# Folding the read-out weights of a state-space scan into the scan's own tables, and building those tables inside the first expert layer

## The chip, the cores and the metric

One core of a Trainium2 chip. The time is device time of one execution in microseconds (us). The kernel before took 613.54 us, the median of 3 runs (612.56 to 614.28).

## The reference

4096 tokens of 256 numbers go through three layers, in fp32:

```
x = x + 0.5 * ffn(layernorm(x))        # 8 experts, one of them per token
x = x + ssm(layernorm(x))              # the recurrence
x = x + 0.5 * ffn(layernorm(x))        # the same experts again

ssm:  Bu_t = B_disc @ u_t              # 128 complex states
      h_t  = a_disc * h_{t-1} + Bu_t   # elementwise
      y_t  = Re(C @ h_t)
ffn:  e = argmax(softmax(x @ Wr)), p = its probability
      out = p * (gelu(x @ W1[e] + b1[e]) @ W2[e] + b2[e])    # 256 -> 1024 -> 256
```

## The kernel before

Everything stands in one program of five instruction streams that wait on one another's semaphores; the order on each engine is written out by hand. It has four stages.

**Entry** (to about 85 us): weights are loaded and split into two fp16 parts each, and the tokens are sorted by expert.

**First expert layer** (`ffn(1)`, about 85 to 303 us). 39 tiles, numbered q. 32 of them hold 128 tokens; seven narrow ones, of 112 down to 16 tokens, hold the rest of each expert. The narrow tiles of 80, 64, 48 and 32 tokens stand at q = 18, 23, 28 and 33, so between full ones, and those of 112, 96 and 16 tokens are the last three. For a tile TensorE turns the tokens (L1245), makes the first product (L1270, 48 matmuls) and the second (L1292 to L1294, 24 matmuls). In iteration q it issues: turn tile q+2, first product of q+1, second product of q. ScalarE does the gelu (L617). VectorE does in iteration q, in this order: `split_x(q+2)` (L950, what the first product of q+2 waits for), `split_h(q+1)` (L964 and L967 for each half, which wait for the gelu of q+1 and are waited for by the second product of q+1), and `result(q)` (L981 to L988: scale, add, statistics of the next layernorm). The result lies in one of two buffers `og`, and GpSimd scatters it to memory by an indirect DMA (L430); `result(q)` waits until the scatter of q-2 has landed. GpSimd also fetches the tokens of tile q+6 (L424).

**Recurrence** (about 303 to 375 us). The 4096 tokens are 8 chunks (`c`) of 512. The states are not complex numbers that turn but two real scans per chunk: the input is turned by a table `turn` (cosines and sines of the angle times the place in the chunk), scanned with the factor `rho` = |a_disc|, and turned back by a table `back`, which also holds B_disc's factor. VectorE does in chunk c: multiply `turn` by the input that TensorE made (L1121, 2 x 512), two scans (L1124), scores and `add_y` of chunk c-1 (L1096 to L1105), the product with `back` (L1133, 2 x 512), and the sum of the two halves into `hr` (L1136). GpSimd makes the start values of chunk c+1 from the ends of the scans (L468 to L474). TensorE does in chunk c: input of c+1 (`into_states`, L1372), turning of chunk c+2 (L1359), scores of chunk c from the normed tokens (L1387, which waits for `add_y(c-1)`), and the read-out of `hr` (L1404).

The tables are made on VectorE in `ffn(1)`: `double(n)` (L774 to L781) makes entries n to 2n of `turn` from the first n. Those for n = 1 to 32 run after `result(q)` for q = 4, 6, ..., 14; those for n = 64, 128 and 256 and the two `readout` calls, which make `back` (L783 to L788), run after the loop's last tile.

**Routing and second expert layer** (about 375 to 611 us): as the first, without tables and statistics.

## Time and profile before

| | |
|---|---|
| median of the timed runs | 613.54 us |
| the profiled execution | 613.17 us |
| its span, first to last instruction | 611.4 us |
| granted TensorE clock, mean | 0.926 of full |
| TensorE busy | 551.8 us, 90% |
| VectorE busy | 467.6 us, 76% |
| GpSimd busy | 288.1 us, 47% |
| stretch of the first expert layer | about 85 to 303 us |
| stretch of the recurrence, first multiply to last scores | 317.13 to 375.0 us |

PE is TensorE, PEld its weight loads, DVE VectorE, ACT ScalarE, POOL GpSimd, SP SyncE. "L1124" is line 1124 of the kernel before. `banks` is PSUM, and `weights_arena` the large buffer in which nearly all tiles lie. Durations of matmuls are modelled at their ends, so times between starts are the safer reading for TensorE.

### The profile page before, as it was taken

What the parts mean: (1) busy time and instruction counts of PE and PEld (TensorE: products, weight loads), DVE (VectorE), ACT (ScalarE), POOL (GpSimd) and SP (SyncE); (2) the same over time, 40 slices, a digit from 0 to 9 for tenths busy, and PEclk for the clock granted to TensorE, in tenths of its full rate; (3) what the DMA queues carried; (4) which work ended last, traced back from release to release, by engine and by line L of the source; (5) the groups of instructions that cost most, each with busy time, mean ns of one, the idle gap of its engine ahead of it and who ended that gap; (6) DMA issues with size and microseconds to landing.
All of it is one profiled execution on the core that took longest, in us unless ns stands there. A gap on an engine that the chain in (4) does not pass through costs nothing.

```text
span 611.4 us, 18700 instructions
## 1 busy us (share of the span) xinstructions
PE 551.8 (90%) x6548; PEld 508.6 (83%) x6548; DVE 467.6 (76%) x1007; ACT 409.8 (67%) x966; POOL 288.1 (47%) x326
## 2 busy tenths in 40 slices
PE   5992158999999999999989989699999999999996
PEld 5991047999999999999977767699999999999996
DVE  5789997888887788877749998666677666666674
ACT  3899977676667776676455662387766677766763
POOL 0025075655655555653245142655555555545532
PEclk9555569999999999999999996799999999999999
DMA  7999112211111121111081223111111112111210
GB/s 250 369 370 378 33 26 97 62 47 55 54 45 55 37 52 44 46 47 36 16 278 35 93 80 104 58 46 54 52 48 53 51 48 45 46 46 46 52 30 15
DMA packets 34873, 51.94 MB, mean 85 GB/s; under 512 B 6747, under 2 KB 27933, under 8 KB 34528
## 3 DMA queue, kind: packets, MB, share of 16 engines
q1 hardware_dynamic: 24800, 31.93, 15.3%
q0 software_dynamic: 9984, 18.83, 11.4%
q8 instruction: 56, 0.92, 0.6%
q14 instruction: 33, 0.27, 0.2%
HBM read 37.98 MB, written 14.59 MB: 86 GB/s over the span
## 4 chain that ended last, share of the span: by engine, by line
PE 67%; DVE 11%; issue 6%; DMA 6%; SPq 4%; POOL 4%; ACT 1%; POOLq 0%; DVEq 0%; ACTq 0%
PE banks L1270 30%; PE banks L1292 10%; PE banks L1293 10%; PE banks L1294 10%; DVE weights_arena L1124 3%; PE banks L1245 3%; DMA weights_arena<-L_attn_u 2%; PE banks L1200 2%; SPq L330 2%; DMA weights_arena<-x_after_ffn 2%; DVE weights_arena L1133 1%; POOL weights_arena L424 1%; DVE weights_arena L1121 1%; SPq L313 1%; DVE weights_arena L1105 1%
## 5 line engine op out<-in xcount | busy, mean ns | idle before, releaser
L617 ACT ACTIVATE weights_arena<-banks,b1t,inv 128x128 f32<-128x128 f32 (+7 forms) x624 | 220.1, 459 | 31.3 <-PE banks L1270 31.2
L1270 PE MATMUL banks<-weights_arena 128*128 128x128 f16 (+7 forms) x3744 | 207.0, 215 | 1.2 <-DVE weights_arena L950 1.1
L1270 PEld LDWEIGHTS banks<-weights_arena 128*128 x3744 | 199.9, 98 | 3.5 <-issue 2.5
L1292 PE MATMUL banks<-weights_arena 128*128 (+7 forms) x624 | 170.3, 273 | 0.2 <-issue 0.2
L1294 PE MATMUL banks<-weights_arena 128*128 (+7 forms) x624 | 170.2, 273 | 0.0
L1293 PE MATMUL banks<-weights_arena 128*128 (+7 forms) x624 | 170.2, 273 | 0.0
L964 DVE TENSOR_SCALAR weights_arena<-weights_arena,hscale 128x512 f16<-128x512 f32 (+5 forms) x156 | 74.7, 479 | 76.0 <-ACT weights_arena L617 75.2
L967 DVE SCALAR_TENSOR_TENSOR weights_arena<-weights_arena,hscale 128x512 f16<-128x512 f32 (+5 forms) x156 | 109.9, 704 | 5.6
L591 ACT ACTIVATE weights_arena<-banks,xscale 128x256 f16<-128x256 f32 (+7 forms) x78 | 35.5, 455 | 90.7 <-PE banks L1245 90.7
L424 POOL DMA_INDIRECT recf<-records,sorti x78 | 76.9, 986 | 23.8 <-issue 23.8
L430 POOL DMA_INDIRECT out<-weights_arena,sorti x39 | 39.5, 1014 | 78.4 <-DVE weights_arena L984 70.6
L430 POOL DMA_INDIRECT x_after_ffn<-weights_arena,sorti x39 | 39.9, 1024 | 77.0 <-DVE weights_arena L988 68.6
L1292 PEld LDWEIGHTS banks<-weights_arena 128*128 128x128 f16 (+7 forms) x624 | 62.3, 100 | 7.0 <-issue 0.7
L1294 PEld LDWEIGHTS banks<-weights_arena 128*128 128x128 f16 (+7 forms) x624 | 62.3, 100 | 6.5
L1293 PEld LDWEIGHTS banks<-weights_arena 128*128 128x128 f16 (+7 forms) x624 | 62.3, 100 | 5.7
L424 POOL DMA_INDIRECT weights_arena<-L_attn_u,sorti x39 | 46.2, 1184 | 29.0 <-DVE sorti L928 17.4
L575 ACT ACTIVATE weights_arena<-weights_arena,recf 128x256 f32<-128x256 f32 (+7 forms) x78 | 46.0, 590 | 8.8 <-DMA recf<-records,sorti 8.8
L981 DVE SCALAR_TENSOR_TENSOR weights_arena<-banks,inv,weights_arena 128x256 f32<-128x256 f32 (+7 forms) x78 | 37.6, 483 | 16.1 <-issue 5.9
L424 POOL DMA_INDIRECT weights_arena<-x_after_ssm,sorti x39 | 40.0, 1026 | 15.1 <-issue 11.6
L950 DVE SCALAR_TENSOR_TENSOR weights_arena<-banks,xscale,weights_arena 128x256 f16<-128x256 f32 (+7 forms) x78 | 35.6, 457 | 7.8 <-ACT weights_arena L591 7.0
L984 DVE SCALAR_TENSOR_TENSOR weights_arena<-weights_arena,recf 128x256 f32<-128x256 f32 (+7 forms) x78 | 37.8, 484 | 2.8
L729 DVE SCALAR_TENSOR_TENSOR weights_arena<-weights_arena,wscale 128x2048 f16<-128x2048 f32 x16 | 37.1, 2341 | 2.3 <-ACT weights_arena L516 2.3
(216 smaller groups left out, 639.1 us busy)
## 6 DMA issues: line engine op xcount, KB each, us to landing
weights_arena<-L_ffn_W SPq DMA_DIRECT2D x16, 1024.0 KB, 12.6
weights_arena<-x_after_ffn SPq DMA_DIRECT2D x8, 516.0 KB, 8.4
weights_arena<-L_attn_u SPq DMA_DIRECT2D x8, 512.0 KB, 10.8
x_after_ssm<-weights_arena SPq DMA_DIRECT2D x8, 512.0 KB, 2.9
weights_arena<-L_ffn_b SPq DMA_DIRECT2D x2, 1024.0 KB, 5.2
recf<-records,sorti POOLq DMA_INDIRECT x78, 2.5
weights_arena<-L_attn_u,sorti POOLq DMA_INDIRECT x39, 3.3
x_after_ffn<-weights_arena,sorti POOLq DMA_INDIRECT x39, 2.5
```

Source lines behind the costliest of these rows:

```text
L424: pool.indirect_dma_start(to, None, source, bass.IndirectOffsetOnAxis(ap=sorti[:, slot(q), index:index + 1].bitcast(U32), axis=0)).then_in ...
L430: pool.indirect_dma_start(dst, bass.IndirectOffsetOnAxis(ap=sorti[:, slot(q), 2:3].bitcast(U32), axis=0), og[q % 2] if ph == 1 else og[q % ...
L575: act.activation(xng[q % 2][0:w], xg[q % RING][0:w], ACT.Identity, bias=recf[0:w, q % RING, 0:1], scale=recf[0:w, q % RING, 1:2]).then_inc ...
L617: last = act.activation(hb[q % 2][:, f, 0:width(q)], src, ACT.Gelu, bias=b1t[:, bass.ds(e * FC + f, 1)], scale=inv1[:, bass.ds(e, 1)])
L964: dve.tensor_scalar(hs[q % 2][:, 0, f, of], hb[q % 2][:, f, of], sc, None, ALU.mult) \
L967: dve.scalar_tensor_tensor(hs[q % 2][:, 1, f, of], hb[q % 2][:, f, of], sc, hs[q % 2][:, 0, f, of], ALU.mult, ALU.subtract).then_inc(s["hs ...
L981: dve.scalar_tensor_tensor(o, acc, i2, b2b[0:w, bass.ds(e * D, D)], ALU.mult, ALU.add) \
L984: last = dve.scalar_tensor_tensor(o, o, recf[0:w, q % RING, 2:3], xg[q % RING][0:w], ALU.mult, ALU.add)
L1270: last = pe.matmul(acc[:, f * P:f * P + n_cols], weights[wpart * DC + d], xts[q % 2][:, xpart, d, 0:n_cols], start=(n == 0), stop=(n == 5))
L1292: pe.matmul(acc, hs[q % 2][:, 0, f, of], high, start=(f == 0), stop=False)
L1293: pe.matmul(acc, hs[q % 2][:, 0, f, of], low, start=False, stop=False)
L1294: last = pe.matmul(acc, hs[q % 2][:, 1, f, of], high, start=False, stop=(f == FC - 1))
```

## The change

1. The factors of `back` are applied inside the scans. The table `turn` is multiplied by the read-out weight w_t of its place, and the constant factor `rho` of the scan becomes a table of `rho * w_t / w_(t-1)` (in `back`). What the scan gives is then already weighted, and the product with `back` (L1133) is gone. `hr` is their sum.
2. `hr` of chunk c is made right after the scans of c, ahead of the scores and `add_y` of c-1. As `hr` now reads `zz` itself, the next multiply into `zz` also waits for it (`s_hr`).
3. The start values of the next chunk divide the weights out again: GpSimd's four products use four numbers of a small table `carry`.
4. For this the tables need the inverses of the weights. Weights nearer to zero than 1e-15 get 1e-12 added. All of it, with the doublings of 64, 128 and 256 and both `readout` calls, is done by `tables_after(q)` after `result(q)` for q = 16 to 34 of the first expert layer; after its last tile only a memset of `state` is left.
5. `og` has six buffers (RING) where it had two, in both expert layers; `result(q)` waits for the scatter of q-6.

```diff
-                                            og[q % 2] if ph == 1 else og[q % 2][:, 0:D], None, ...
+                                            og[q % RING] if ph == 1 else og[q % RING][:, 0:D], None, ...
...
-                pool.tensor_tensor(ev[:, 18:19], zr, cl, ALU.mult)
+                pool.tensor_tensor(ev[:, 18:19], zr, carry[:, 0:1], ALU.mult)
...
+            def away_from_zero(part):
+                tmp, weight = aa[:, part, :], back[:, part, :]
+                link(dve.tensor_tensor(tmp, weight, weight, ALU.mult))
+                link(dve.tensor_scalar(tmp, tmp, NEAR_ZERO ** 2, None, ALU.is_lt))
+                link(dve.scalar_tensor_tensor(weight, tmp, STAND_IN, weight, ALU.mult, ALU.add))
+            def inverse_of_both(quarter):
+                of = slice(quarter * CH // 4, (quarter + 1) * CH // 4)
+                link(dve.tensor_tensor(aa[:, 0, of], back[:, 0, of], back[:, 1, of], ALU.mult))
+                link(dve.reciprocal(aa[:, 0, of], aa[:, 0, of]))
+            def inverses(part):
+                link(dve.tensor_tensor(inverse[:, part, :], back[:, 1 - part, :], aa[:, 0, :], ALU.mult))
+            def carries():
+                last = CH - 1
+                ends = inverse[:, :, last]
+                dve.tensor_scalar(carry[:, 0:2], ends, turn[:, 0, last:CH], None, ALU.mult)
+                link(dve.tensor_scalar(carry[:, 2:4], ends, turn[:, 1, last:CH], None, ALU.mult))
+            def weighted_turn(part):
+                link(dve.tensor_tensor(turn[:, part, :], turn[:, part, :], back[:, part, :], ALU.mult))
+            def steps(part):
+                tmp = aa[:, part, :]
+                link(dve.scalar_tensor_tensor(tmp[:, 1:CH], back[:, part, 1:CH], rho[:], inverse[:, part, 0:CH - 1],
+                                              ALU.mult, ALU.mult))
+                link(dve.tensor_scalar(tmp[:, 0:1], back[:, part, 0:1], rho[:], None, ALU.mult))
+                link(dve.tensor_copy(back[:, part, :], tmp))
+            def tables_after(q):
+                if 4 <= q < 16 and q % 2 == 0:
+                    double(1 << (q // 2 - 2))
+                elif q == 16:
+                    double(CH // 8)
+                elif q == 18:
+                    double(CH // 4)
+                elif q in (19, 20):
+                    double(CH // 2, CH // 4 * (q - 19), CH // 4 * (q - 18))
+                elif q in (21, 22):
+                    readout(q - 21)
+                elif q in (23, 24):
+                    away_from_zero(q - 23)
+                elif 25 <= q < 29:
+                    inverse_of_both(q - 25)
+                elif q in (29, 30):
+                    inverses(q - 29)
+                elif q in (31, 32):
+                    if q == 31:
+                        carries()
+                    weighted_turn(q - 31)
+                elif q in (33, 34):
+                    steps(q - 33)
...
-                    if q >= 2:
-                        dve.wait_ge(s["scat"][(q - 2) % RING], (q - 2) // RING * 16 + 16)
+                    if q >= RING:
+                        dve.wait_ge(s["scat"][q % RING], q // RING * 16)
...
-                        if 4 <= q < 16 and q % 2 == 0:
-                            double(1 << (q // 2 - 2))
+                        tables_after(q)
                 if ph == 1:
-                    for n in (CH // 8, CH // 4, CH // 2):
-                        double(n)
-                    dve.memset(state[:], 0.0)
-                    readout(0)
-                    readout(1)
+                    link(dve.memset(state[:], 0.0))
...
                 if c >= 1:
+                    dve.wait_ge(s_hr, c)
                     dve.wait_ge(s_state, c)
                 dve.tensor_tensor(zz, turn[:], both(bank[2]), ALU.mult).then_inc(s_mod, 1)
                 dve.wait_ge(s_mod, c + 1)
                 for part_of in range(2):
-                    scan = dve.tensor_tensor_scan(zz[:, part_of, :], rho[:].to_broadcast([P, CH]), zz[:, part_of, :],
+                    scan = dve.tensor_tensor_scan(zz[:, part_of, :], back[:, part_of, :], zz[:, part_of, :],
                                                   state[:, part_of:part_of + 1], ALU.mult, ALU.add)
                 scan.then_inc(s_scan, 1)
+                if c >= 2:
+                    dve.wait_ge(s_y, c - 1)
+                dve.wait_ge(s_scan, c + 1)
+                dve.tensor_tensor(hr[c % 2], zz[:, 0, :], zz[:, 1, :], ALU.add).then_inc(s_hr, 1)
                 if c >= 1:
                     logits_of(c - 1)
                     add_y(c - 1)
                 else:
                     negative_means(len(BATCHES) - 1)
-                dve.wait_ge(s_scan, c + 1)
-                link(dve.tensor_tensor(zb, zz, back[:], ALU.mult))
-                if c >= 2:
-                    dve.wait_ge(s_y, c - 1)
-                dve.tensor_tensor(hr[c % 2], zb[:, 0, :], zb[:, 1, :], ALU.add).then_inc(s_hr, 1)
```

`link` makes the next VectorE instruction wait for the end of the one it wraps. `double` takes a range now, so that the doubling of 256 runs in two halves of 128 entries.

## Rows read from the trace of the kernel before

**Rows 1.** The page, part 1: busy us (share), instructions.
```profile
PE 551.8 (90%) x6548; PEld 508.6 (83%) x6548; DVE 467.6 (76%) x1007; ACT 409.8 (67%) x966; POOL 288.1 (47%) x326
```

**Rows 2.** Timeline of TensorE, first expert layer: start us, duration us, engine, line, operation.
```profile
210.02 2.85 PE L1270 MATMUL banks<-weights_arena 128*128 128x128 f16 x48
...
215.55 1.56 PE L1270 MATMUL banks<-weights_arena 128*128 128x64 f16 x48
...
219.79 2.84 PE L1270 MATMUL banks<-weights_arena 128*128 128x128 f16 x48
```

**Rows 3.** Timeline of VectorE, same stretch; in brackets idle us before, and the releaser.
```profile
207.72 0.49 DVE L964 TENSOR_SCALAR weights_arena<-weights_arena,hscale 128x512 f16<-128x512 f32 x1 [0.81 <-ACT weights_arena L617]
...
211.94 0.35 DVE L950 SCALAR_TENSOR_TENSOR weights_arena<-banks,xscale,weights_arena 128x128 f16<-128x128 f32 x1
...
217.86 0.48 DVE L950 SCALAR_TENSOR_TENSOR weights_arena<-banks,xscale,weights_arena 128x256 f16<-128x256 f32 x1
```

**Rows 4.** Timeline of VectorE, recurrence: one chunk, and the last chunk's multiply.
```profile
337.36 1.21 DVE L1121 TENSOR_TENSOR weights_arena<-turn,banks 128x1024 f32<-128x1024 f32 x1
338.61 2.46 DVE L1124 TENSOR_TENSOR_SCAN weights_arena<-rho,state,weights_arena 128x512 f32<-128x512 f32 x2
...
341.36 1.21 DVE L1105 TENSOR_TENSOR weights_arena<-weights_arena,banks 128x1024 f32<-128x1024 f32 x1
342.49 1.22 DVE L1133 TENSOR_TENSOR weights_arena<-weights_arena,back 128x1024 f32<-128x1024 f32 x1
343.74 0.69 DVE L1136 TENSOR_TENSOR weights_arena<-weights_arena 128x512 f32<-128x512 f32 x1
...
365.32 1.22 DVE L1121 TENSOR_TENSOR weights_arena<-turn,banks 128x1024 f32<-128x1024 f32 x1
```

**Rows 5.** Timeline of TensorE, recurrence: chunk 0, then a later chunk.
```profile
320.91 1.04 PE L1359 MATMUL banks<-ident,weights_arena 128*128 128x128 f32 x8
321.78 1.85 PE L1387 MATMUL banks<-wrc,weights_arena 128*128 128x8 f32 x16
323.52 2.06 PE L1404 MATMUL banks<-ct,weights_arena 128*128 128x265 f32 x8
...
344.50 2.05 PE L1404 MATMUL banks<-ct,weights_arena 128*128 128x265 f32 x8
346.38 1.88 PE L1372 MATMUL banks<-weights_arena,bt 128*128 128x512 f32 x4
348.10 1.04 PE L1359 MATMUL banks<-ident,weights_arena 128*128 128x128 f32 x8
```

**Rows 6.** Timeline of GpSimd, start value of chunk 1.
```profile
321.62 1.16 POOL L473 TENSOR_TENSOR state<-ev 128x1 f32<-128x1 f32 x1
```

**Rows 7.** Timeline of VectorE after the first expert layer: `double` and `readout`.
```profile
303.71 0.29 DVE L778 TENSOR_SCALAR back<-turn 128x128 f32<-128x128 f32 x1
...
304.88 0.35 DVE L778 TENSOR_SCALAR back<-turn 128x256 f32<-128x256 f32 x1
...
306.46 0.48 DVE L787 TENSOR_SCALAR weights_arena<-turn,ev 128x512 f32<-128x512 f32 x1
...
307.76 0.49 DVE L787 TENSOR_SCALAR weights_arena<-turn,ev 128x512 f32<-128x512 f32 x1
```

**Rows 8.** Groups of VectorE by line and form: count, busy us, mean ns, idle before.
```profile
L722 DVE RECIPROCAL wscale<-bound 128x2 f32<-128x2 f32 x8 | 1.3, 166 | 0.3
L916 DVE RECIPROCAL records<-records 128x32 f32<-128x32 f32 x2 | 0.7, 356 | 0.1
```

**Rows 9.** VectorE waiting ahead of L964, 188.9 to 290 us: total us, times.
```profile
  ACT weights_arena L617: 12.5, 17
```

**Rows 10.** Timelines, end of the first expert layer: VectorE's result of the 96-token tile, TensorE.
```profile
299.52 0.48 DVE L981 SCALAR_TENSOR_TENSOR weights_arena<-banks,inv,weights_arena 96x256 f32<-96x256 f32 x1 [1.86 <-DMA x_after_ffn<-weights_arena,sorti]
...
300.66 10.98 PE L1178 MATMUL banks<-iota_r,ident 128*128 128x128 f32 x96
```

**Rows 11.** Busy time of TensorE by stretch: us, busy, granted clock, DMA share, GB/s.
```profile
368.00:370.00 2.00, 2.00 (x12) 0.50 0.00 0
```

More of the change, by code:

```diff
@@ L55 @@
 TINY = 1e-30
+NEAR_ZERO = 1e-15
+STAND_IN = 1e-12
 WE = DC * F
@@ L119, in macaron @@
         state = sb("state", [P, 2])
+        carry = sb("carry", [P, 4])
         wsum = sb("wsum", [P, NW])
@@ L177, in macaron @@
         hs = [view(4096 + k * 1024, 2, FC, P, dt=F16) for k in range(2)]
-        og = [view(6144 + k * RW, RW) for k in range(2)]
+        og = [view(6144 + k * RW, RW) for k in range(RING)]
         xg = [view(8192 + k * D, D) for k in range(RING)]
@@ L181, in macaron @@
         xts = [view(10240 + k * 256, 2, DC, P, dt=F16) for k in range(2)]
-        outcols = [view(6912 + k * D, DC, P) for k in range(2)]
+        outcols = [view(12288 + k * D, DC, P) for k in range(2)]
         xs = view(0, NJ, RW)
@@ L188, in macaron @@
         zz = view(NJ * RW + 2 * CT * D + 2 * DC * CH, 2, CH)
-        zb = view(NJ * RW + 2 * CT * D + 2 * DC * CH + 2 * CH, 2, CH)
+        inverse = view(NJ * RW + 2 * CT * D + 2 * DC * CH + 2 * CH, 2, CH)
         hr = [view(NJ * RW + 2 * CT * D + 2 * DC * CH + 4 * CH + k * CH, CH) for k in range(2)]
@@ L430, in scatter @@
                     pool.indirect_dma_start(dst, bass.IndirectOffsetOnAxis(ap=sorti[:, slot(q), 2:3].bitcast(U32), axis=0),
-                                            og[q % 2] if ph == 1 else og[q % 2][:, 0:D], None, bounds_check=T - 1, oob_is_err=False) \
+                                            og[q % RING] if ph == 1 else og[q % RING][:, 0:D], None, bounds_check=T - 1, oob_is_err=False) \
                         .then_inc(s["scat"][q % RING], 16)
@@ L467, in _ @@
                 pool.wait_ge(s_scan, c + 1)
-                pool.tensor_tensor(ev[:, 18:19], zr, cl, ALU.mult)
-                pool.tensor_tensor(ev[:, 19:20], zi, cl, ALU.mult)
-                pool.tensor_tensor(ev[:, 20:21], zi, sl, ALU.mult)
-                pool.tensor_tensor(ev[:, 21:22], zr, sl, ALU.mult).then_inc(s_prod, 1)
+                pool.tensor_tensor(ev[:, 18:19], zr, carry[:, 0:1], ALU.mult)
+                pool.tensor_tensor(ev[:, 19:20], zi, carry[:, 1:2], ALU.mult)
+                pool.tensor_tensor(ev[:, 20:21], zi, carry[:, 3:4], ALU.mult)
+                pool.tensor_tensor(ev[:, 21:22], zr, carry[:, 2:3], ALU.mult).then_inc(s_prod, 1)
                 pool.wait_ge(s_prod, c + 1)
@@ L772, in rotation, with double @@
                 link(dve.tensor_scalar(turn[:, 1, 0:1], col(11), col(13), None, ALU.mult))
-            def double(n):
-                c0, s0 = turn[:, 0, 0:n], turn[:, 1, 0:n]
+            def double(n, begin=0, end=None):
+                end = n if end is None else end
+                c0, s0 = turn[:, 0, begin:end], turn[:, 1, begin:end]
                 cn, sn = turn[:, 0, n - 1:n], turn[:, 1, n - 1:n]
-                dve.tensor_scalar(back[:, 0, 0:n], s0, sn, None, ALU.mult)
-                link(dve.tensor_scalar(back[:, 1, 0:n], c0, sn, None, ALU.mult))
-                dve.scalar_tensor_tensor(turn[:, 0, n:2 * n], c0, cn, back[:, 0, 0:n], ALU.mult, ALU.subtract)
-                link(dve.scalar_tensor_tensor(turn[:, 1, n:2 * n], s0, cn, back[:, 1, 0:n], ALU.mult, ALU.add))
+                dve.tensor_scalar(back[:, 0, begin:end], s0, sn, None, ALU.mult)
+                link(dve.tensor_scalar(back[:, 1, begin:end], c0, sn, None, ALU.mult))
+                dve.scalar_tensor_tensor(turn[:, 0, n + begin:n + end], c0, cn, back[:, 0, begin:end], ALU.mult, ALU.subtract)
+                link(dve.scalar_tensor_tensor(turn[:, 1, n + begin:n + end], s0, cn, back[:, 1, begin:end], ALU.mult, ALU.add))
             def readout(part):
@@ L975, in result @@
                     dve.wait_ge(s["m2"], q + 1)
[L976 to L977 removed]
+                    if q >= RING:
+                        dve.wait_ge(s["scat"][q % RING], q // RING * 16)
                     w = width(q)
[L979 removed]
+                    o, acc = og[q % RING][0:w, 0:D], bank[4 + q % 2][0:w, 0:D]
                     i2 = inv2[0:w, bass.ds(e, 1)]
@@ L987, in result @@
                         link(dve.bn_stats(stats[0:w, q % 2, :], o))
-                        last = dve.bn_aggr(og[q % 2][0:w, D:D + 2], stats[0:w, q % 2, :])
+                        last = dve.bn_aggr(og[q % RING][0:w, D:D + 2], stats[0:w, q % 2, :])
                     last.then_inc(s["o"], 1)
```

2 lines of the change are left out of this document (removed).

## The prediction, made before the changed kernel was run

> **What bounds the kernel now.** I read the busy times first [rows 1]: TensorE is busy for 90% of the span, VectorE for 76%. That is a mean over stages, so I went on to the timelines of the two stages that the change touches.
>
> In the first expert layer TensorE sets the pace. The first products start at 210.02 and 215.55 (5.53 us for a full tile), and 4.24 us later at 219.79 behind the 64-token tile [rows 2]. VectorE needs less: of a full tile's 5.5 us it waits 0.81 for the gelu [rows 3]. `split_x` runs ahead of its product. The one at 211.94 ends at 212.29, 3.26 us before the product at 215.55 that needs it; behind a narrow tile the lead is short, 218.34 against 219.79, so 1.45 us [rows 2, 3]. These leads are the cover for anything that makes VectorE late.
>
> In the recurrence VectorE sets the pace, with no idle time that a row names: multiply 1.25 us (start to start), two scans 2.46, scores and `add_y` to 342.49, the product with `back` 1.25, `hr` 0.69. From the multiply at 337.36 (chunk 3) to the one at 365.32 (chunk 7) four periods pass, 6.99 us each [rows 4]. TensorE has slack, but not much. Its four groups take, start to start, 1.88 (read-out), 1.72 (input), 0.87 (turning, from chunk 0, where the next group doesn't wait) and 1.74 (scores): 6.21 us [rows 5].
>
> **The recurrence after the change.** The product with `back` goes: 1.25 us per chunk, so VectorE's own period becomes 5.74. TensorE's is 6.21 and is late next, so it gives the new pace. I walked both through the chunks. The read-out of chunk 0 stays at 323.52, as the scores ahead of it already fill TensorE [rows 5]. `hr` is ready earlier, but the first `add_y` comes after it and holds the next scores: multiply of chunk 1 at about 322.5 (its start value, ready at 322.9 behind an operation of 1.22, now comes behind `hr`'s 0.69 [rows 4, 6]), its `hr` done 4.35 later, scores and `add_y` 1.6 more, 328.4; the read-out of chunk 1 then starts near 330.3, where it now would be 323.52 + 6.99 = 330.5. From there the period is 6.21: read-outs at 336.5, 342.7, 348.9, 355.1. The multiply of chunk 7 needs the input product, which starts 1.88 after the read-out of chunk 5 and, with its end and the semaphore, is there some 2.1 later: 359.1. Before it was 365.32, gain 6.2. Behind it lie only VectorE's scans, `hr`, `add_y` and routing, shorter by one more 1.25: **gain 7.4 us**. Were VectorE the bound throughout, it would be 8 x 1.25 = 10.0. If TensorE's period were 6.4 it would be 6.4.
>
> The moved `hr` and the new wait for it cost nothing: `add_y` stands between `hr` and the next multiply. The start value must be there too. GpSimd's six small products usually take 1.1 us behind the scans, but while VectorE ran a product of two SBUF operands one of them took 1.16 instead of some 0.2 [rows 6]. `hr` is such an operation and now starts together with them: 0.69 + 1.1 = 1.8 us, against 0.61 + 0.37 + 1.13 = 2.1 until the next multiply. It is hidden, by 0.3; past the first chunk TensorE gives another 0.4.
>
> The scans get a table where they had one broadcast number. No row shows a scan so fed. A product of two fp32 operands takes 0.69 for 512 against 0.48 with one [rows 4, 7], so up to 0.21 per scan, 0.42 per chunk; a gain has no reason. I take 0: a scan runs at 1.23 per 512 [rows 4], slower than either. The other end gives a VectorE period of 6.16, still under TensorE's 6.21, and only the last chunk's 0.4 and the first's are paid, about 1 us.
>
> The Trainium skill ("DVE: opcode table, instruction layouts, handler registers and perf-mode slots", section 6) says that the built-in scan runs at half throughput because its result is fed back. The two scans' 2.46 us for 1024 elements, against 1.21 for the multiply of as many [rows 4], agree; by that rule the second table is hidden, by the other end it costs the 1 us above.
>
> **The tables in the first expert layer.** Each call is priced to the next start in its chain, with 0.1 for restarting `split_x` behind a chained end:
> - q = 16: doubling of 64, between 0.9 and 1.17: 1.0. q = 18, 19, 20: doublings over 128 entries, 304.88 - 303.71 = 1.17, so 1.27 each [rows 7].
> - q = 21, 22: `readout`, 307.76 - 306.46 = 1.30, so 1.4 each [rows 7].
> - q = 23, 24: product 0.69, comparison 0.48, and the multiply-add 0.75 that is in `readout`'s 1.30; with gaps 2.1 each.
> - q = 25 to 28: product of 128 (0.28) and a reciprocal of 128. The trace has reciprocals of 2 columns at 0.166 and of 32 at 0.356 [rows 8]: 6.3 ns a column, 0.96 us for 128. 1.4 each. Below, a plain operation's 0.29 for 128 [rows 7] would make 0.7; above, 1.6.
> - q = 29, 30 0.8 each; q = 31 1.15; q = 32 0.8; q = 33, 34 (multiply 0.75, a small one, copy 0.48) 1.6 each.
>
> The sum is 24.2 us in 19 tiles. Before, the part of it that already existed (three doublings and two `readout`s) ran after the layer while TensorE waited for the reload of the tokens, and was hidden. Room in the layer: VectorE waits for the gelu 12.5 us in this stretch [rows 9], and I add an estimate of 0.1 for each of these 17 waits, where it could start at once: 14 to 15 us. The difference is some 9.5 us.
>
> The leads don't store that. I carried the lateness from tile to tile, adding each call, subtracting each wait, and letting TensorE wait where lateness exceeds the lead less an estimated 0.4 for restarting it. It passes until q = 20 (2.5 late against 2.8); then TensorE waits behind the narrow tile at 23 (1.5), for tiles 26, 27, 28 (1.0, 1.0, 0.7), behind 28 (2.0), for 31 (0.3), behind 33 (1.2) and for 37 (0.3): **8.0 us**, and 0.9 of lateness goes into the tail. Work 10% less or more makes it 5.8 or 10.4; 20% less, 3.9.
>
> **The six buffers.** Only one wait for a scatter shows, at the 96-token tile: 1.86 us [rows 10]. Behind it the last result follows, and everything waits for its scatter. Two results of 1.7 us from 299.52 end at 302.9. TensorE's last product ends at 300.66 [rows 10], so the last result can end at 302.4: gain 0.5, of which the lateness may eat some. I take 0.3. In the second layer the last results wait for TensorE: 0. What ran after the layer (6.3 us) frees VectorE at a time when nothing needs it: 0.
>
> **The sum.** +8.0 - 0.3 - 7.4 = +0.3 us. The profiled execution took 613.17, its span 611.4 with 1.8 around it, 0.4 under the median; on the median 613.5 the sum gives 613.8.
>
> **The rivals.**
> - *The tables fit.* If VectorE does the calls in 80% of my price (a quicker reciprocal, short chained gaps), TensorE waits 3.9 us, not 8.0. Time 609.7. For it: q = 14's doubling today costs nothing at all. Against it: the account of VectorE's time doesn't close unless much of the 24.2 us is overpriced. A clock that holds to the end of the recurrence (now 0.50 at 368 [rows 11]) could add up to 1 us. Chance, for all that ends under 611.7: 0.32.
> - *TensorE's clock falls in the expert layer* (the slower side). Now it is at the full level through the layer, without idle time. With eight waits of 0.3 to 2 us it may fall as it does near 368, after a stretch with gaps and small products. At 0.50 each 8 us of products take 8 more, of which VectorE's lateness pays back its wait, some 4: 613.8 + 4 = 617.8. It decides from the first wait over 1 us, at tile 24. Against it: in the recurrence the clock stays at the full level with two gaps in each 7 us. Chance 0.12.
> - *The calls cost 10% to 15% more* (two-operand products held up, reciprocals at 1.2): TensorE waits 10.4 or more: 616.2. Chance, with the scans' 1 us, 0.17.
> - *The change doesn't do what it says:* scans fed by a table run at 1.44 each. As worked out, 614.8, because TensorE hides most. This lies inside the likeliest case's own range.
>
> On the second of these the Trainium skill ("TensorE: Matmul & The Clock Gate", section on HAM oscillation) warns that idle gaps between bursts of matmuls throttle the engine again; by that rule the time is the 617.8 of that case. No row here shows a fall inside an expert layer.
>
> **How the numbers follow.** About 0.3% (1.8 us) is what a measurement of this kernel can tell from no change. The likeliest case, the two sides cancel, has 0.39 and the range 611.7 to 615.4. Faster is the first rival, 0.32 (its bound with both ends: 3.9 waits and 8.5 gain, 608.6). Slower is 0.12 + 0.17 = 0.29, to 618. The range 609.5 to 618 leaves out the ends of both.
>
> **What would show it.** No group of products with `back` in the recurrence, periods of 6.2 there with TensorE waiting nowhere; the last scores about 7.4 us closer to the first multiply. In the first expert layer VectorE without waits for the gelu from q = 18 on, and TensorE's first products waiting for `split_x`, most of all behind the narrow tiles; the layer's last product some 8 us later. The prediction is wrong if TensorE's products keep their 5.5 us through q = 34, or if the recurrence runs at 5.8.

## The result, and the profile after

The kernel after takes 615.45 us (median of 15 runs, 613.48 to 617.39), the one before, measured beside it, 613.24 (15 runs). The ratio is 1.0032 with a 95% interval of 1.0020 to 1.0044: slower, by 2.2 us, just beyond the 0.3% that I had called the limit of what can be told. I had forecast +0.3 us, and 615.45 lies 0.05 above the range 611.7 to 615.4 that I had given to the likeliest case. Single executions of one kernel differ by 1 to 2 us with how TensorE's clock behaved in the first 20 us, which the last section shows.

The profiled execution took 616.36 us. Its page, the span and part 1 (busy us, share, instructions), to be held against [rows 1]:

```profile
span 614.6 us, 18732 instructions
PE 551.8 (90%) x6548; PEld 508.2 (83%) x6548; DVE 471.9 (77%) x1029; ACT 410.8 (67%) x966; POOL 289.9 (47%) x326
```

Nothing there says what happened: the busy times are the same within 1%, though eight products of 1.22 us are gone and a table is built. The stages say it. I cut both spans at the same instructions, from the timelines (us; the differences are my subtraction):

| stretch | before | after | difference | forecast |
|---|---|---|---|---|
| start to the first product of tile 2 (q = 2) | 99.88 | 101.46 | +1.58 | 0 |
| first expert layer, from there to TensorE's last product | 200.78 | 208.47 | +7.69 | +8.0 |
| from there to the first multiply of the recurrence | 16.47 | 16.37 | -0.10 | -0.3 |
| first multiply to the last (chunk 0 to 7) | 48.19 | 43.70 | -4.49 | -6.2 |
| last multiply to the last scores | 9.41 | 8.37 | -1.04 | -1.25 |
| routing, to the first product of the second expert layer | 22.38 | 21.84 | -0.54 | 0 |
| to the end | 214.29 | 214.39 | +0.10 | 0 |
| span | 611.4 | 614.6 | +3.2 | +0.3 |

The first row is not the change: nothing ahead of that product was edited, and the same stretch takes 99.81 or 101.27 us in two kernels below whose code there is identical (experiments 2 and 3; the last section gives the cause). What is left, 1.6 us, is the change by the traces; the medians say 2.2.

**The layer.** TensorE's first products of tiles 22, 23 (the narrow one), 24 and 26 (the first of them answers to the one at 210.02 in [rows 2]); the bracket is idle time and releaser:

```profile
211.61 2.85 PE L1329 MATMUL banks<-weights_arena 128*128 128x128 f16 x48
217.13 1.61 PE L1329 MATMUL banks<-weights_arena 128*128 128x64 f16 x48
223.21 2.85 PE L1329 MATMUL banks<-weights_arena 128*128 128x128 f16 x48 [1.62 <-DVE weights_arena L1014]
...
235.44 2.85 PE L1329 MATMUL banks<-weights_arena 128*128 128x128 f16 x48 [0.75 <-DVE weights_arena L1014]
```

Behind the narrow tile the next product comes 6.08 us later, where it was 4.24 [rows 2]: 1.84 more. The bracket names `split_x` (L1014) as what it waited for. The waits of the whole layer, after (us in all, times, longest):

```profile
PE banks L1329 <- DVE weights_arena L1014: 6.9, 6, 1.9
DVE weights_arena L1028 <- ACT weights_arena L619: 8.4, 8, 3.6
```

Of the first line 0.5 us, one wait near the layer's start, stood in before too. The second line is VectorE's spare time in 100 to 312 us; by the same view of 190 to 305 alone it has none left, where before had the 12.5 us of [rows 9]. The groups of VectorE in 190 to 305 us say it too (idle before it, at the end of the line):

```profile
L1028 DVE TENSOR_SCALAR weights_arena<-weights_arena,hscale 128x512 f16<-128x512 f32 (+6 forms) x40 | 19.4, 484 | 0.4 <-issue 0.3
```

**The recurrence.** VectorE, the last periods before and after the wait (start, duration, idle and releaser):

```profile
349.81 1.22 DVE L1181 TENSOR_TENSOR weights_arena<-turn,banks 128x1024 f32<-128x1024 f32 x1
351.06 2.46 DVE L1184 TENSOR_TENSOR_SCAN weights_arena<-back,state,weights_arena 128x512 f32<-128x512 f32 x2
...
355.97 1.22 DVE L1181 TENSOR_TENSOR weights_arena<-turn,banks 128x1024 f32<-128x1024 f32 x1
...
362.14 1.22 DVE L1181 TENSOR_TENSOR weights_arena<-turn,banks 128x1024 f32<-128x1024 f32 x1
363.39 2.46 DVE L1184 TENSOR_TENSOR_SCAN weights_arena<-back,state,weights_arena 128x512 f32<-128x512 f32 x2
...
370.00 1.22 DVE L1181 TENSOR_TENSOR weights_arena<-turn,banks 128x1024 f32<-128x1024 f32 x1 [1.80 <-POOL state L476]
```

The period is 6.16 to 6.17 us, where it was 6.99 [rows 4]. The scan that reads a table takes 2.46 for two, as before. But the last multiply comes 7.86 after the one before it, and waits 1.80 us for the start value. TensorE's groups run back to back (the transposes and scores of the chunk, left out here, fill 361.94 to 364.52):

```profile
358.35 2.03 PE L1463 MATMUL banks<-ct,weights_arena 128*128 128x265 f32 x8
360.22 1.88 PE L1431 MATMUL banks<-weights_arena,bt 128*128 128x512 f32 x4
...
364.52 2.03 PE L1463 MATMUL banks<-ct,weights_arena 128*128 128x265 f32 x8
```

364.52 - 358.35 = 6.17: TensorE sets the pace of the recurrence now. VectorE is close behind it: from its multiply at 355.97 to the end of `add_y` at 362.04 it takes 6.07, and the next multiply starts at 362.14, when the input product (360.22 + 1.88 = 362.10) is there. What held the start value is on GpSimd:

```profile
363.68 1.00 POOL L460 TENSOR_SCALAR m<-m 128x16 f32<-128x16 f32 x1 [2.44 <-ACT banks L661]
364.77 3.80 POOL L461 TENSOR_TENSOR records<-m,mhalf 128x16 f32<-128x16 f32 x1
368.64 0.23 POOL L462 TENSOR_TENSOR records<-nmean,records 128x16 f32<-128x16 f32 x1
368.82 0.19 POOL L470 TENSOR_TENSOR ev<-weights_arena,carry 128x1 f32<-128x1 f32 x1
...
369.68 0.19 POOL L476 TENSOR_TENSOR state<-ev 128x1 f32<-128x1 f32 x1
```

These first three are `second_norm`, the norm factors of the first half of the tokens, put on GpSimd's queue ahead of the start value of chunk 7. The scans it needs had ended at 365.85; it could begin only at 368.82. Before, the same three instructions (L457 to L459 there) stood in the same place of the queue:

```profile
356.82 0.94 POOL L457 TENSOR_SCALAR m<-m 128x16 f32<-128x16 f32 x1 [0.67 <-ACT banks L659]
357.84 3.35 POOL L458 TENSOR_TENSOR records<-m,mhalf 128x16 f32<-128x16 f32 x1
361.27 0.80 POOL L459 TENSOR_TENSOR records<-nmean,records 128x16 f32<-128x16 f32 x1
...
362.97 0.19 POOL L474 TENSOR_TENSOR state<-ev 128x1 f32<-128x1 f32 x1
```

They ended at 362.07, and the scans of that chunk at 362.04, so they held up nothing. The start value was ready at 363.16 and its multiply ran at 365.32 [rows 4], 2.2 us later, and no list of waits of the multiply named GpSimd.

Why are they 3 us later against the scans in after? They start when ScalarE has the squares that they need. TensorE's input product of chunk 6 and the last of these squares, in before, and then the last of the squares in after:

```profile
353.37 1.88 PE L1372 MATMUL banks<-weights_arena,bt 128*128 128x512 f32 x4
356.54 0.19 ACT L659 ACTIVATION_READ_ACCUMULATOR banks<-weights_arena,nmean 128x1 f32 x1
```

```profile
363.40 0.20 ACT L661 ACTIVATION_READ_ACCUMULATOR banks<-weights_arena,nmean 128x1 f32 x1
```

In before the squares were ready 1.6 us ahead of the multiply of chunk 6 (356.73 against 358.33), in after 1.5 behind it (363.60 against 362.14). ScalarE does them behind its copies of TensorE's results, so it keeps step with TensorE; and TensorE lost its lead over VectorE: its input product ended 3.1 us ahead of that multiply in before (355.25), and 0.04 ahead of it in after (362.10).

### The profile page after: what moved, and what is told of

Read it like the earlier page. It is cut to its first block, busy times and chain, and to the rows that moved or that the text cites. A ratio compares the mean times of both kernels' runs of the same rounds, so it can differ in the third digit from the quotient of the medians.

```text
span 614.6 us, 18732 instructions
## 1 busy us (share of the span) xinstructions
PE 551.8 (90%) x6548; PEld 508.2 (83%) x6548; DVE 471.9 (77%) x1029; ACT 410.8 (67%) x966; POOL 289.9 (47%) x326
## 4 chain that ended last, share of the span: by engine, by line
PE 70%; DVE 11%; issue 6%; POOL 5%; DMA 3%; ACT 2%; DVEq 1%; SPq 1%; ACTq 0%; POOLq 0%
PE banks L1329 27%; PE banks L1351 10%; PE banks L1353 9%; PE banks L1352 9%; PE banks L1259 4%; PE banks L1304 2%; PE banks L1231 2%; PE banks L1431 1%; POOL weights_arena L427 1%; DVE weights_arena L1031 1%; PE banks L1446 1%; DVE weights_arena L1028 1%; DMA recf<-records,sorti 1%; PE banks L1463 1%; DMA weights_arena<-x_after_ffn 1%
## 5 line engine op out<-in xcount | busy, mean ns | idle before, releaser
L1014 DVE SCALAR_TENSOR_TENSOR weights_arena<-banks,xscale,weights_arena 128x256 f16<-128x256 f32 (+7 forms) x78 | 35.6, 456 | 10.3 <-ACT weights_arena L593 6.9
```

## The experiments

All were measured beside the kernel before, whose median was 614.20 in the set of experiments 1 to 4 (28 runs), 613.21 in that of 5 to 8 (23) and 614.58 in that of 9 and 10 (17). The experiments have 4 to 12 runs each. Every ratio is to it. My account has two claims: the tables cost 7 to 8 us because VectorE is late behind narrow tiles, and the missing gain of the recurrence is `second_norm`. The rivals: each call costs TensorE its time wherever it stands; and the recurrence lost its time to `hr` and the new order.

**1. `second_norm` one chunk later.**

```diff
-                if c == NC - 3:
+                if c == NC - 2:
                     pool.wait_ge(s_sq, NC // 2)
                     second_norm(slice(0, NJ // 2))
```

> The changed kernel, but GpSimd makes the first half of the second norm's factors behind the start value of chunk 7, not ahead of it. Theory A (that work of some 5 us, which fitted into a period of 7 us, now holds up the start value by the 1.80 us that VectorE waited ahead of the last multiply): the last multiply comes 43.70 - 1.8 = 41.9 us after the first, the wait is gone, and the time is 1.5 to 1.8 us under the changed kernel's 615.45: 613.8. Rival B (VectorE would wait for TensorE's input product there anyway): the wait changes its releaser, under 0.3 us gained.

613.57 us, ratio 0.9984 (0.9969 to 0.9998). From the first multiply to the last it is now 41.80 us, where after has 43.70 and my walk had 41.97. GpSimd in this kernel, last chunks: the start value first, the norm factors behind it.

```profile
364.85 0.19 POOL L470 TENSOR_TENSOR ev<-weights_arena,carry 128x1 f32<-128x1 f32 x1 [4.69 <-DVE weights_arena L1184]
364.99 0.64 POOL L471 TENSOR_TENSOR ev<-weights_arena,carry 128x1 f32<-128x1 f32 x1
...
366.13 0.19 POOL L476 TENSOR_TENSOR state<-ev 128x1 f32<-128x1 f32 x1
366.41 0.21 POOL L460 TENSOR_SCALAR m<-m 128x16 f32<-128x16 f32 x1
366.71 2.91 POOL L461 TENSOR_TENSOR records<-m,mhalf 128x16 f32<-128x16 f32 x1
369.70 1.27 POOL L462 TENSOR_TENSOR records<-nmean,records 128x16 f32<-128x16 f32 x1
```

So 1.9 us of the recurrence were this wait. Nothing else was edited. The start value is ready at 366.32, 0.9 us ahead of its multiply at 367.22: of the 2.2 us of room in before, 0.9 are left.

**2. The table calls spread over the layer from q = 1.**

```diff
-                if 4 <= q < 16 and q % 2 == 0:
-                    double(1 << (q // 2 - 2))
-                ...
+                if 1 <= q < 9:
+                    double(1 << (q - 1))
+                elif q in (9, 10):
+                    double(CH // 2, CH // 4 * (q - 9), CH // 4 * (q - 8))
+                elif q in (12, 13):
+                    readout(q - 12)
+                elif q in (15, 17):
+                    away_from_zero((q - 15) // 2)
+                elif q in (19, 20, 22, 24):
+                    inverse_of_both((19, 20, 22, 24).index(q))
+                elif q in (25, 27):
+                    inverses((q - 25) // 2)
+                elif q == 29:
+                    carries()
+                    weighted_turn(0)
+                elif q == 30:
+                    weighted_turn(1)
+                elif q == NT - 1:
+                    steps(0)
+                    steps(1)
```

> The changed kernel with the same tables, but the calls begin at q = 1 instead of 4, the wide doublings at 7 to 10 instead of 16 to 20, and the last step (two calls) comes after the layer's last tile. Theory A (the loss in the first expert layer is an account of VectorE's time: 24 us of calls in tiles that have 15 us of room; the tiles from 1 to 15 have some 0.9 us each that stood empty): TensorE waits 1 to 2 us in place of 7.7, the stretch from its second first-product to its last product is 190.5 against 196.6, and the time is some 6 us under 615.45: 609.5. Rival B (each call costs TensorE time by itself, by its chained gaps or by memory contention, wherever it stands): the stretch stays at 196 or more and the time at 615.

612.42 us, ratio 0.9961 (0.9945 to 0.9978). The layer takes 204.20 us, 4.3 less than after and 3.4 more than before. The calls are the same, only their places differ, so "each costs TensorE its time wherever it stands" falls. But I had expected 6. Waits were left at eight tiles (11 to 24), by the starts of the first products 0.83 us at the largest and 3.4 in all. The prices are hardly to blame, as in after the calls came out as forecast (next section); so the account had too much room or too long leads in these tiles, and which of the two is not shown.

**3. Both.** The edits of 1 and 2 together.

> Both edits together: GpSimd's norm factors behind the last start value, and the table calls spread from q = 1. Theory A: the two add up, 615.45 - 6 - 1.7 = 607.8, so 5.5 under the kernel before. Rival B (a saving in the recurrence is given back by the routing behind it): 609.5, as the spreading alone.

611.01 us, ratio 0.9942 (0.9921 to 0.9964), where the sum of the two had promised 607.8. The layer is 204.11, as in 2. The recurrence shows something new: 45.16 us from the first multiply to the last, not 41.8. TensorE there (start, duration), and then by stretch (length, busy, granted clock, share and GB/s of DMA):

```profile
327.86 2.03 PE L1461 MATMUL banks<-ct,weights_arena 128*128 128x265 f32 x8
...
335.27 3.88 PE L1461 MATMUL banks<-ct,weights_arena 128*128 128x265 f32 x8
338.94 3.11 PE L1429 MATMUL banks<-weights_arena,bt 128*128 128x512 f32 x4
```

```profile
332.00:336.00 4.00, 3.33 (x23) 0.82 0.38 131
336.00:340.00 4.00, 4.00 (x10) 0.50 0.00 0
340.00:344.00 4.00, 4.00 (x24) 0.82 0.39 131
```

The granted clock fell from 2.4 to 1.2 GHz for some 7 us, and the read-out took 3.88 us for 2.03. As TensorE sets the pace now, that is 3.4 us of this execution. Most runs can't have had it: of the twelve, four (the profiled one, 613.17, among them) took 613.2 to 613.5 and the other eight 607.7 to 611.7, and the median lies 1.4 under experiment 2, near the 1.9 of `second_norm`.

**4. The tables alone:** the layer of after, the recurrence of before. The last four calls (`weighted_turn` and `steps`, two each) write to a place that nothing reads.

```diff
-                link(dve.tensor_tensor(turn[:, part, :], turn[:, part, :], back[:, part, :], ALU.mult))
+                link(dve.tensor_tensor(unused[:, part, :], turn[:, part, :], back[:, part, :], ALU.mult))
...
-                link(dve.tensor_copy(back[:, part, :], tmp))
+                link(dve.tensor_copy(unused[:, part, :], tmp))
...
+                link(dve.tensor_tensor(zb, zz, back[:], ALU.mult))
```

> The kernel before in its recurrence (product with back, old carries, old order), with the changed kernel's table calls at the same tiles and the six buffers; the last table writes go to an unused buffer. Theory A (the tables cost 7.7 us in the first expert layer, and the recurrence gave back 5.5): stretch of the first expert layer 196.6, recurrence with periods of 6.99, time 613.24 + 7.7 - 0.3 = 620.6. Rival B (part of the loss is from elsewhere in the change, such as six buffers or code layout): the layer shows less than 196, the time is under 619.

621.18 us (4 runs), ratio 1.0105 (1.0075 to 1.0135): 7.0 us slower by the medians. The layer takes 208.38, the recurrence 48.20, each as in the kernel that it comes from.

**5. The change without its tables.** The calls from q = 16 on are memsets of the three tables, so the recurrence computes with other numbers.

```diff
                 elif q == 16:
-                    double(CH // 8)
+                    link(dve.memset(turn[:, :, CH // 8:CH], 0.5))
                 elif q == 18:
-                    double(CH // 4)
+                    link(dve.memset(back[:], 0.5))
...
```

> The changed kernel without the table calls from q = 16 on: three memsets stand in for them, and the tables hold a constant, so the output of the recurrence is another; what is measured is the time of everything else. Theory A (the layer's 7.7 us are these calls alone): the first expert layer is as long as in the kernel before, the recurrence keeps the changed kernel's 43.7 us from the first to the last multiply, time 615.45 - 7.7 = 607.8. Rival (part of the layer's loss is due to the six buffers or another change): over 609.

608.50 us, ratio 0.9914 (0.9891 to 0.9938). The layer is 200.78, as before to the last digit, and the recurrence 43.49. All four runs are of the slower of the two kinds in the last section; against the ten runs of before of that kind in this set (614.40) they are 5.9 us faster, which is what the stages give, 4.7 in the recurrence and 1.0 behind it. (The trace is of the slowest of the four, and has 1.5 us more in the first tile of the second expert layer, as that of experiment 2 has and no other.) 4 and 5 together: the tables cost what the layer grew by, 7.6 to 7.7 us, and the rest of the change gives back 5.9.

**6. Six result buffers alone**, on the kernel before.

```diff
-        og = [view(6144 + k * RW, RW) for k in range(2)]
+        og = [view(6144 + k * RW, RW) for k in range(RING)]
...
-                    if q >= 2:
-                        dve.wait_ge(s["scat"][(q - 2) % RING], (q - 2) // RING * 16 + 16)
+                    if q >= RING:
+                        dve.wait_ge(s["scat"][q % RING], q // RING * 16)
```

> The kernel before with six result buffers and nothing else. Theory A: only the wait of 1.86 us at the 96-token tile goes, and TensorE's last product then bounds the last result, so the reload begins 0.3 to 0.4 us earlier: 613.24 - 0.3 = 612.9, same within the measurement. Rival (the whole wait of 1.86 us is gained): 611.4.

613.36 us, ratio 1.0000 (0.9986 to 1.0015). From the last product to the first multiply its trace has 16.19 us, 0.28 less than before, which is the size of my term; the comparison can't show so little. (Its trace has 10.71 us from the last multiply to the last scores, where before has 9.41: its granted clock was 0.51 in 364 to 380 us.)

**7. `hr` in its old place**, behind `add_y`, all else as in after.

```diff
-                ...
-                dve.tensor_tensor(hr[c % 2], zz[:, 0, :], zz[:, 1, :], ALU.add).then_inc(s_hr, 1)
                 if c >= 1:
                     logits_of(c - 1)
                     add_y(c - 1)
                 ...
+                dve.tensor_tensor(hr[c % 2], zz[:, 0, :], zz[:, 1, :], ALU.add).then_inc(s_hr, 1)
```

> The changed kernel with hr made behind the scores and add_y of the chunk before, its old place. Theory A (TensorE sets the period of 6.17 us and needs hr only some 4 us after the scans, while the early hr mainly holds up add_y): the periods stay at 6.2 and the time within 0.5 us of 615.45. Rival (the early hr is what lets TensorE run without gaps): periods of 6.5 and more, over 617.

613.17 us, ratio 0.9993 (0.9979 to 1.0006), so some 2 us under after. I had not expected that. The stages give 1.2 of it: 42.71 to the last multiply, 8.20 behind it. The periods end at 6.17 as in after (the early ones are 0.9 longer in all than in experiment 1); what differs is `second_norm`:

```profile
362.85 0.21 POOL L460 TENSOR_SCALAR m<-m 128x16 f32<-128x16 f32 x1 [2.29 <-ACT banks L661]
363.14 2.92 POOL L461 TENSOR_TENSOR records<-m,mhalf 128x16 f32<-128x16 f32 x1
366.14 0.24 POOL L462 TENSOR_TENSOR records<-nmean,records 128x16 f32<-128x16 f32 x1
```

3.5 us instead of 5.2, and the last multiply waits for nothing: `hr` ends at 367.97, the start value is ready before it, the multiply runs at 368.06. `second_norm` starts during VectorE's multiply of 361.89 and not inside a scan; the last section says why that matters. The other 1 us of the medians' difference is in none of these stages and stays open; in the two traces 0.75 of it lies ahead of tile 2, where the code is the same.

**8. The calls fitted to the spare time**, and `second_norm` later. Twenty calls go to places with room by the account, and the last five run behind the last tile, while the reload of the tokens is under way.

```diff
-                ...
+                calls = [lambda k=k: double(1 << k) for k in range(8)]
+                ...
+                places = (1, 2, 3, 4, 5, 6, 8, 9, 11, 13, 14, 17, 19, 22, 25, 28, 29, 32, 33, 34)
+                if q in places:
+                    calls[places.index(q)]()
+                elif q == NT - 1:
+                    carries()
+                    for part in range(2):
+                        weighted_turn(part)
+                    for part in range(2):
+                        steps(part)
```

> GpSimd's norm factors behind the last start value, and the table calls placed by the account of lateness: 20 calls at q = 1 to 34 so that none pushes VectorE past its leads, with 0.15 us more per call than priced, and the five last (5 us) behind the layer's last tile, where VectorE waits 6.9 us for the reload. Theory A: TensorE waits nowhere in the first expert layer (length as before the change, 7.7 us under the changed kernel's), the recurrence runs as in the first of these experiments (41.8 us to the last multiply): 615.45 - 7.7 - 1.9 = 605.9. Rival (the account is too coarse, as the spread version's 3.4 us of waits against 1.8 show): 2 us of waits are left, 608. A half-rate stretch of TensorE inside the recurrence, as one traced run of the second kind had, would add up to 3.4 us to single runs of either.

605.15 us (5 runs), ratio 0.9870 (0.9847 to 0.9893): faster than before and than every kernel so far. The medians differ by 8.1 us; four of the five runs are of the faster kind of the last section, and against the twelve runs of before of that kind (612.64) their median, 605.11, is 7.5 lower. The layer is 200.75 us, the recurrence 42.17. TensorE's products around the narrow tile keep the distances of [rows 2], 5.53 and 4.24:

```profile
211.06 2.85 PE L1322 MATMUL banks<-weights_arena 128*128 128x128 f16 x48
216.59 1.56 PE L1322 MATMUL banks<-weights_arena 128*128 128x64 f16 x48
220.83 2.84 PE L1322 MATMUL banks<-weights_arena 128*128 128x128 f16 x48
```

And behind the layer VectorE ends the last table and then still waits for the reload:

```profile
307.83 0.43 DVE L827 COPY back<-weights_arena 128x512 f32<-128x512 f32 x1
...
310.36 0.20 DVE L1165 TENSOR_SCALAR nb<-weights_arena 128x4 f32<-128x4 f32 x1 [1.98 <-DMA weights_arena<-x_after_ffn]
```

**9. Experiment 8 with `hr` in its old place**, by the edit of 7.

> The fitted version (20 calls where the account has room, five behind the layer, GpSimd's norm factors behind the last start value), with hr made behind add_y, in its old place. Theory C (the changed kernel with hr in its old place gained 1.2 us in its trace because the norm factors on GpSimd ran 3.2 us there and 5.0 with the early hr, and so held up the last start value less; with the factors moved away nothing is left to gain): within 0.5 us of the fitted version's 605.15. Rival (the late hr gains by itself, through the start values' products that it no longer stretches): 603.5 to 604.

605.65 us (6 runs), ratio 0.9854 (0.9827 to 0.9880). The same as 8 within the intervals. So no gain from the place of `hr` can be told once `second_norm` is out of the way; what it gave in 7 came, as far as the stages show it, by way of that queue. (Its profiled execution had a granted clock of 0.60 in 320 to 324 us, and 44.31 us to the last multiply.)

**10. `second_norm` later in the kernel before**, by the edit of 1.

> The kernel before with GpSimd's first norm factors behind the start value of chunk 7 and nothing else. Theory A (in a period of 6.99 us that work was hidden: the start value was ready 2.2 us before the multiply): no change, 613.2. Rival (the work cost something there too): 612 or less.

614.79 us, ratio 1.0005 (0.9987 to 1.0024), and 48.17 us to the last multiply, where before has 48.19. In the kernel before the place of these three instructions costs nothing. The change made it cost 1.9 us.

## Why the prediction was right or wrong

**The tables: right, for the reason given.** +7.69 us against +8.0. The calls from q = 16 to 34, each taken from the last instruction of `result` to the next `split_x` and less the same distance in before, add up to 23.5 us, where I had 24.2; none is more than 0.13 off. The starts of the first products show where (my subtraction against before): tile 24, behind the narrow one, 1.84 (forecast 1.5), 26 0.92 (1.0), 27 1.05 (1.0), 28 0.25 (0.7), 29 2.04 (2.0), 31 none (0.3), 34 1.32 (1.2), 37 0.25 (0.3). The account of lateness against lead holds here, though in experiment 2 it was 1.6 us too hopeful, and experiment 8, placed by it with 0.15 us more per call, took all of the waits away. Of the prices the one from furthest off held: the reciprocal of 128, worked out at 0.96 from [rows 8]. VectorE in after:

```profile
246.09 0.95 DVE L804 RECIPROCAL weights_arena<-weights_arena 128x128 f32<-128x128 f32 x1
```

**The pace of the recurrence: right.** TensorE is late next, at 6.17 (forecast 6.21). VectorE's own 5.74 was too low: its chain fills 6.07 of the 6.17, because `hr`, now right behind the scans, starts 0.1 us after their end, where scores started ahead of it. TensorE hid that. The scans cost nothing more; the first two multiplies lie 5.46 apart (5.37), the second with 0.9 us of waiting for its start value, which `hr` holds up. Without the wait of the last chunk the stretch is 41.80 (41.97).

**What failed is one step:** "Behind it lie only VectorE's scans, `hr`, `add_y` and routing", with the start value that "is hidden, by 0.3; past the first chunk TensorE gives another 0.4". I had priced GpSimd's six small products and not read what else stood on its queue. `second_norm` took 5.2 us there (356.82 to 362.07) and held up nothing, since it ended with the scans. In after it ends 3.0 us behind them, because the squares it needs come later against VectorE, and the start value's room is down from 2.2 us to 0.9; 1.80 us came out. The forecast of -6.2 became -4.49. Put into my sum, the 1.9 us make +2.2. That this is also the difference of the medians is partly luck: the stages of the two traces, without the first, add up to 1.6, as routing gave 0.54 that I had not forecast and the layer, the buffers and the tail were each off by 0.2 to 0.3. Experiment 1 shows the step alone, 8 and 9 without the other loss, and 10 that in the kernel before it costs nothing.

**The tail: 0.2 short.** 8.37 for 9.41 is 1.04, where I had 1.25.

**The buffers: of no effect that can be told.** -0.10 in after, -0.28 alone in experiment 6, where I said 0.3. In after the lateness of VectorE may take back part: it ends the last result 1.87 us after TensorE's last product.

**Routing: not forecast.** -0.54 us. The granted clock is 0.50 in its first 2.3 us in before and in its first 0.7 in after; how much of the 0.54 that makes is not shown. I had put up to 1 us of this into the rival "the tables fit".

**The rivals.** *The tables fit* did not happen in the kernel as changed, as the calls cost 3% less than priced and not 20% less; but it is possible, as experiment 8 shows. *TensorE's clock falls in the expert layer* did not happen. Its granted clock from 209 to 262 us, with 5.3 us of waits in it:

```profile
209.00:262.00 53.00, 47.69 (x657) 1.00 0.16 43
```

The section of the Trainium skill that I had set beside it ("TensorE: Matmul & The Clock Gate", on HAM oscillation) warns of idle gaps between bursts of matmuls, and I had read 617.8 out of it. Its own case has waits for DMA, longer than any wait of this layer; gaps of up to 2.0 us did not lower the clock in any layer profiled here, so that use of it was too wide, and longer gaps no run here tests. The fall that did come (experiment 3) was in the recurrence, in small products. *The calls cost 10% to 15% more* was near the truth in time (616.2) and not in cause: they cost 3% less. *Scans at 1.44* did not happen.

## What to carry to other kernels

When a stage gets a shorter period, list everything that stands on every engine's queue inside it, once-only work too, with what it waits for and its slack against the consumer: what was hidden by 2.2 us of slack names itself in no list of waits. When the bound moves from one engine to another, the old lead of the new one is gone (3.1 us here), and all that keeps step with it comes later against the rest. Work given to an engine that runs ahead of a bottleneck costs nothing up to its lead and its full time beyond, so it belongs in many small places ahead of the wide tiles, and what is left over behind the last one, where a reload covers it. And when a saving moves the bound to TensorE, its clock becomes part of the price.

## What the runs showed of the hardware that I had not expected

**GpSimd is held where it starts inside a VectorE operation with two SBUF operands.** In after, L460 starts at 363.68, inside the first scan (363.39 to about 364.62), and takes 1.00, up to 364.68; the same instruction takes 0.21 in experiment 1. L461, started at 364.77 inside the second scan (to 365.85), takes 3.80 for 2.91. In experiment 1 L462 starts at 369.70 and ends at 370.97, with this scan:

```profile
368.48 2.46 DVE L1184 TENSOR_TENSOR_SCAN weights_arena<-back,state,weights_arena 128x512 f32<-128x512 f32 x2
```

which ends at 370.94. And L471 takes 0.64 for 0.19 when `hr` runs. In experiment 7 L461 started 0.01 us ahead of the scans and took 2.92 right through them, and L460 took 0.21 beside a multiply whose second operand is in PSUM. The Trainium skill ("SBUF — State Buffer", section "SBUF: two separate sides") says that the two engines share a pair of ports as an exclusive lock, which a VectorE operation with two SBUF inputs takes against a GpSimd operation that reads SBUF. The trace agrees for GpSimd, in the kernel before as well: L459 starts at 361.27 inside a scan, takes 0.80, and ends at 362.07, where the scans end at 362.04. The page's other half, that VectorE is blocked when GpSimd starts first, is not what the trace shows: in experiment 1 L461 ran from 366.71 to 369.62, and the scans that start inside it, at 368.48, kept their 2.46. The measurement decides.

**One stretch of full clock at the start makes two kinds of execution.** The stretch up to tile 2 takes 99.81 to 100.16 us in the six profiled executions whose mean granted clock is 0.92 to 0.93, and 100.71 to 101.46 in the six with 0.99. So those with the higher mean are the slower, by 1.2 us from median to median. The timed runs say the same of one kernel: before's with the higher mean are 1.0, 1.8 and 2.2 us slower than its others in the three sets. TensorE's scores of 16 products in before, at 12 us, at 25 us and at the end of the recurrence, where the granted clock is 0.50 [rows 11]:

```profile
12.16 1.93 PE L1200 MATMUL banks<-wrc,weights_arena 128*128 128x8 f32 x16
...
24.74 3.42 PE L1200 MATMUL banks<-wrc,weights_arena 128*128 128x8 f32 x16
...
367.88 3.42 PE L1387 MATMUL banks<-wrc,weights_arena 128*128 128x8 f32 x16
```

And the same scores in after:

```profile
13.23 3.56 PE L1259 MATMUL banks<-wrc,weights_arena 128*128 128x8 f32 x16
...
28.41 3.42 PE L1259 MATMUL banks<-wrc,weights_arena 128*128 128x8 f32 x16
```

By stretch (length, then busy us and instructions of PE, PEld, DVE, ACT and POOL, then the granted clock), before and after:

```profile
20.00:40.00 20.00, 18.61 (x88) 18.12 (x88) 15.12 (x43) 18.25 (x20) 0.00 (x0) 0.50 1.08 366
```

```profile
20.00:40.00 20.00, 20.00 (x97) 20.00 (x98) 14.81 (x43) 18.95 (x20) 0.00 (x0) 1.00 1.08 365
```

3.42 us is the duration at 0.50, and 1.85 that at 1.00 [rows 5]. So from 20 us on TensorE ran at the lower level in both, whatever the column says: the 1.00 of after can't be what it ran at. The real difference is at 12 us, where before had some 3 us of full clock (1.93) and after had not (3.56). The other profiles agree: at 12 us the products of this group follow each other in 112 ns in all six of the lower mean, and in 213 ns in all six of the higher. An execution with that stretch has its scores 1.6 us sooner and the eight transposes behind them 0.9; it then waits for data where the other does not (1.4 us by 35 us in before), and some 1.2 are left. So where the mean granted clock is compared between executions, it has to be held against durations first; and a difference between two single traces of this kernel carries 1 to 2 us that are not the code's. What decides whether the stretch comes stays open.

**The clock can fall inside the recurrence** (experiments 3, 4, 6 and 9 of the twelve profiles: 0.50 in 336 to 340 us, 0.57 in 360 to 364, 0.57 in 330 to 334, 0.60 in 320 to 324), at different places in kernels whose code there is nearly the same. It cost some 2 us in experiment 9 (44.31 against 42.17 in 8) and 3.4 in 3, where TensorE is the bound, and 0.0 and 0.3 in 4 and 6, where VectorE is. What sets it off stays open.
